# Three self-attentions of a four-layer Perceiver kernel, laid out anew by head group and half batch

## The chip, the cores and the metric

The kernel runs on one core of a Trainium2 chip. The metric is the time of one execution on the device in microseconds (us). A profiled execution has a span, from its first to its last instruction, and a time of its own that also counts what lies around the span.

## The reference, cut to what matters

A tensor of 32 batches x 32 tokens x 128 features goes through four layers, each a cross-attention to a context of 257 tokens, a self-attention and a feed-forward block. Each self-attention has 16 heads of 8 features; it is made of the shapes below. Layer 0 has a linear attention that the change leaves alone. The three others are:

```python
# layer 1: causal, 16 query heads, 4 key and value heads; x normalised before
# layer 2: attends over the head axis in a transposed reading ("pairs"): tokens and
#          features are regrouped first; a relative position bias is ADDED TO THE PROBABILITIES
# layer 3: plain softmax attention; a second layer norm of the already normalised x
#          is added to the result with the projection's bias
s = einsum('bhqd,bhkd->bhqk', q, k) * 8 ** -0.5   # + causal mask in layer 1
p = softmax(s)                                     # + relative bias in layer 2
o = einsum('bhqk,bhkd->bhqd', p, v) @ Wo           # + residual
```

All of it is in float32.

## The kernel before, in words

The 1024 token rows live as 8 tiles of 128 rows (X, XN, Y, Z, ACC), and transposed, features by tokens, as XNT, ZT and OT. PSUM is one tile PS of 8 banks of 512 columns. Each engine has its own program (`@block.tensor`, `.scalar`, `.vector`, `.gpsimd`, `.sync`), written out by hand; a named semaphore in `sig` stands between every producer and consumer, and a `Tally` counts what each engine waits for. So the order of the work on an engine is exactly the order of the calls. There is no planner.

A self-attention in the token layers starts from the layer norm of the carried sum in banks 6 and 7 (`norm` on ACT for the tiles 0 to 3, `layernorm` on DVE for 4 to 7), eight transposes (`turn`, line 440) and two copies to XNT, the first half by ACT and the second by DVE. Then:

- PE projects queries and keys 512 columns at a time (`wide`, line 464) and values by token tile (line 818). ACT copies all three out of PSUM (lines 1035, 1289, 1291).
- `heads` on DVE spreads the queries: for each batch the 32 queries are written four times, masked by head, so that a group of four heads (32 rows) makes 4 x 32 columns.
- `core` on PE (line 794) makes the scores: for each half (16 batches), head group g of four and batch one 32x32 stationary of keys against 128 columns of queries. 128 matmuls; PE issues each float32 matmul as two records.
- The scores stand keys by queries. `core` on DVE transposes them in 32x32 blocks (line 1831), adds the mask, takes the maximum, subtracts; ACT takes the exponential of a half (2048 columns); DVE sums, divides (POOL does half of it in `divide`, line 2276), transposes back (lines 1859, 1870).
- `core` on PE (line 805) multiplies the values, 128 matmuls of 32x32 by 128 columns, into all eight banks; ACT and DVE pick each head out of its four (line 1877) and ACT copies to OT (lines 1271, 1278). Only then PE carries X into banks 6 and 7 (`carry`, line 456) and projects (line 472).

In the pair attention ACT stages q, k and v (1024 columns each), SP and ACT send 16 transfers to another layout (`to_pairs`, 8 each), ACT copies the parts (line 1382), `core(pairs=True)` runs, and 16 transfers bring the result back (`to_tokens`, on ACT, SP and POOL). While the first transfers are under way DVE builds the relative bias from one-hot rows (line 2097 and the products before it). In layer 3 DVE also makes the second norm between the transposes and `heads` (lines 2165 to 2171).

## Time and profile before

| | us |
|---|---|
| median of 3 runs (1364.64 to 1371.31) | 1369.34 |
| profiled execution, its own time | 1370.04 |
| its span | 1368.2 |
| PE busy in it | 1136.3 |
| DVE busy | 772.6 |
| ACT busy | 593.1 |
| POOL busy | 327.8 |

PE is TensorE's matmul records, PEld its weight loads, which overlap them; DVE is VectorE, ACT ScalarE, POOL GpSimd, SP the queue of transfers. Matmuls are pipelined and their ends are modelled, so a busy PE need not be at its peak. The mean granted clock of TensorE is 0.884 of full speed; it has two levels, 1.2 and 2.4 GHz, shown as 0.50 and 1.00. L794 is line 794 of the kernel before.

### The profile page before, as it was taken

How to read it: one execution, taken by the hardware profiler on the slowest of the kernel's cores; microseconds unless marked ns; L12 is line 12 of the kernel's file. 1: busy time of each engine (PE TensorE's matmuls, PEld its weight loads, DVE VectorE, ACT ScalarE, POOL GpSimd, SP SyncE). 2: the span in 40 equal slices, each digit the busy share in tenths (PEclk: the TensorE clock that was granted, in tenths of full speed). 3: DMA queues.
4: the chain of work that ended last, by engine and by line, in shares of the span. 5: the costliest groups of instructions: out<-in, count | busy, mean ns of one | idle time of the engine just before them, and what ended most of it. 6: DMA issues, size and time to landing. Idle time of an engine off the chain costs nothing.

```text
span 1368.2 us, 26696 instructions
## 1 busy us (share of the span) xinstructions
PE 1136.3 (83%) x8831; PEld 834.3 (61%) x8831; DVE 772.6 (56%) x2093; ACT 593.1 (43%) x1233; POOL 327.8 (24%) x504
## 2 busy tenths in 40 slices
PE   5768998999998368899986046799999989999538
PEld 2435665877785345688864034577777768887435
DVE  2375445555553953687775495534334357776783
ACT  2153223433433223677764212544344347776223
POOL 1010001112120004455531010304041315554110
PEclk8587999999999578999997556899999999999658
DMA  8510111222230002355510301021211211111000
GB/s 284 144 62 1 36 58 28 58 59 53 54 72 1 1 1 87 85 151 152 142 58 1 46 1 39 24 58 47 58 47 47 58 36 28 31 31 36 2 1 16
DMA packets 71006, 75.05 MB, mean 55 GB/s; under 512 B 6288, under 2 KB 63712, under 8 KB 70552
## 3 DMA queue, kind: packets, MB, share of 16 engines
q1 hardware_dynamic: 67880, 66.18, 17.9%
q0 software_dynamic: 1152, 6.97, 1.4%
q10 hardware_dynamic: 1904, 0.98, 0.5%
q8 instruction: 43, 0.70, 0.2%
q14 instruction: 27, 0.22, 0.1%
HBM read 71.49 MB, written 0.52 MB: 53 GB/s over the span
## 4 chain that ended last, share of the span: by engine, by line
PE 74%; DVE 14%; ACT 5%; DMA 3%; issue 2%; ACTq 1%; POOL 1%; SPq 0%; DVEq 0%; POOLq 0%
PE PS L487 13%; PE PS L499 12%; PE PS L877 9%; PE PS L717 4%; PE PS L887 4%; DVE AR L1436 4%; PE PS L681 4%; PE PS L464 2%; PE PS L724 2%; PE PS L668 2%; PE PS L490 2%; PE PS L860 2%; PE PS L867 2%; PE PS L907 2%; PE PS L440 2%
## 5 line engine op out<-in xcount | busy, mean ns | idle before, releaser
L499 PEld LDWEIGHTS PS<-WB,AR 128*128 128x128 f32 x1568 | 190.5, 193 | 43.6 <-issue 38.8
L499 PE MATMUL PS<-WB,AR 128*128 128x128 f32 x1568 | 190.7, 276 | 0.0
L1035 ACT ACTIVATE AR<-PS,WB 128x512 f32<-128x512 f32 x160 | 110.0, 687 | 155.0 <-PE PS L487 148.2
L877 PE MATMUL PS<-AR 128*128 128x257 f32 x512 | 138.6, 393 | 1.7 <-POOL AR L2307 1.6
L1561 DVE SCALAR_TENSOR_TENSOR ACC<-PS,SM,ACC 128x128 f32<-128x128 f32 x192 | 54.1, 345 | 95.1 <-PE PS L499 94.1
L487 PE MATMUL PS<-ZT,WB 128*128 128x512 f32 x208 | 100.9, 608 | 0.3 <-ACT AR L1035 0.3
L877 PEld LDWEIGHTS PS<-AR 128*128 128x128 f32 x512 | 87.1, 190 | 21.4 <-issue 7.2
L1436 DVE TENSOR_TENSOR AR<-PS,AR 128x512 f32<-128x512 f32 (+2 forms) x69 | 48.4, 701 | 90.1 <-issue 39.3
L487 PE MATMUL PS<-XNT,WB 128*128 128x512 f32 x168 | 89.1, 638 | 5.2 <-ACT AR L1035 4.1
L1035 ACT ACTIVATE AR<-PS 128x512 f32<-128x512 f32 (+2 forms) x82 | 44.3, 541 | 112.9 <-PE PS L490 68.0
L1035 ACT ACTIVATE AR<-PS,SM 128x257 f32<-128x257 f32 x136 | 64.6, 475 | 38.7 <-DVE SM L1644 28.8
L1561 DVE SCALAR_TENSOR_TENSOR X<-PS,SM,X 128x128 f32<-128x128 f32 x168 | 47.2, 344 | 59.2 <-PE PS L499 58.8
L805 PE MATMUL PS<-AR 32*32 32x128 f32 x768 | 31.4, 374 | 58.0 <-DVE AR L1870 57.5
L887 PE MATMUL PS<-W,AR 128*128 128x128 f32 x512 | 76.8, 273 | 1.5 <-ACT AR L1035 1.4
L1035 ACT ACTIVATE AR<-AR 128x1024 f32<-128x1024 f32 (+1 forms) x39 | 46.3, 1188 | 71.2 <-DVE AR L1436 56.1
L887 PEld LDWEIGHTS PS<-W,AR 128*128 128x128 f32 x512 | 63.4, 141 | 15.1 <-ACT AR L1035 2.6
L2307 POOL TENSOR_TENSOR AR<-AR,W 128x512 f32<-128x512 f32 x64 | 67.0, 1047 | 19.9 <-POOL OT L2335 13.4
L1035 ACT ACTIVATE AR<-AR,SM 128x257 f32<-128x257 f32 x128 | 65.3, 510 | 14.7 <-DVE SM L1983 9.4
L2257 POOL TENSOR_TENSOR AR<-AR,SM 128x516 f32<-128x516 f32 x32 | 33.7, 1054 | 156.8 <-ACT SM L1035 93.9
L794 PE MATMUL PS<-AR 32*32 32x128 f32 x768 | 27.9, 416 | 47.0 <-DVE AR L1436 45.9
L440 PE MATMUL PS<-W,XN 128*128 128x128 f32 x96 | 29.7, 397 | 44.6 <-ACT XN L1035 44.3
L805 PEld LDWEIGHTS PS<-AR 32*32 32x32 f32 x768 | 26.2, 147 | 63.5 <-DVE AR L1870 61.0
(266 smaller groups left out, 2246.0 us busy)
## 6 DMA issues: line engine op xcount, KB each, us to landing
WB<-in_units SPq DMA_DIRECT2D x49, 385.0 KB, 3.1
CTX<-in_fside SPq DMA_DIRECT2D x32, 514.0 KB, 4.1
CTX<-in_ctxT SPq DMA_DIRECT2D x96, 130.0 KB, 2.1
CTX<-in_ctxT SPq DMA_DIRECT2D x8, 520.0 KB, 4.8
CTX<-in_ctxN SPq DMA_DIRECT2D x16, 258.0 KB
CTX<-in_ctxN SPq DMA_DIRECT2D x32, 129.0 KB, 2.3
AR<-in_ctxN SPq DMA_DIRECT2D x32, 64.5 KB, 2.9
AR<-in_l1x_w POOLq DMA_DIRECT2D x1, 2048.0 KB, 8.4
```

What stands on the lines that cost most here:

```text
L440: m = pe.transpose(PS[:, t // 4, 128 * (t % 4):128 * (t % 4) + 128], src[:, t, :], ident)
L487: m = pe.matmul(bank(2 * c), WB[:, q, 128 * c:128 * c + 128], src[:, 512 * hh:512 * hh + 512], start=True, stop=True)
L499: m = pe.matmul(PS[:, 4 + hh, 128 * t:128 * t + 128], f_h[hh][:, c, 128 * t:128 * t + 128], WB[:, q, 2 * UNIT + 128 * c:2 * UNIT + 128 * c ...
L681: m = pe.matmul(bank(1 + c), c_T[k][:, P * c:P * c + P], rhs, start=True, stop=True)
L717: m = pe.matmul(o, y_P[q][:, c, P * g:P * g + P], c_N[k][:, c, :], start=(c == 0), stop=(c == 1))
L805: m = pe.matmul(PS[32 * g:32 * g + 32, 4 * half + b, P * tt:P * tt + P], c_vt[32 * b:32 * b + 32, at:at + 32], pt[32 * b:32 * b + 32, g, t ...
L877: m = pe.matmul(PS[:, 2 + g, 0:KEYS], x_qb[q][:, P * g:P * g + P], x_k[q], start=True, stop=True)
L887: m = pe.transpose(PS[:, 6 + pair, 256 * c + P * (g % 2):256 * c + P * (g % 2) + P], x_p[q][:, g, P * c:P * c + P], ident)
L1035: return act.activation(o, i, fn, **k)
L1436: return dve.tensor_tensor(o, a, b, op)
L1561: ins = dve.scalar_tensor_tensor(out=a, in0=y, scalar=f_w[:, 4 * hh + t, bass.ds(e, 1)], in1=a, op0=ALU.mult, op1=ALU.add)
L2307: pool.tensor_tensor(x_qb[q].rearrange("p (h q) -> p h q", h=H), qv, m16, ALU.mult)\
```

## The change

Scores are made queries by keys, so that a row of PSUM is a query and the softmax runs along rows with no 32x32 transposes. For that the keys, not the queries, are spread by head (ACT copies with a scale column, `c_keys`). The work is cut into 8 units u: a half of the batches and a head group, 512 columns each. DVE takes maximum and difference straight out of PSUM, ACT the exponential, DVE the sums; PE transposes the unit in four 128x128 steps (`c_turn`), ACT copies it. Values are projected per batch and head (`c_values` on PE), spread to a block form by POOL (`spread_values`), and PE weighs them with the turned exponentials (`c_weigh`). The division comes last: the reciprocals are transposed and spread by PE over the output's layout (`c_turn_sums`, `c_spread`) and DVE multiplies (`c_close`). The causal mask is written by PE into PSUM before the scores add to it. The bias of the pair attention becomes a product of its own (`c_pair_bias`) from a table that POOL builds early. The second norm of layer 3 is derived from the first one's variance, and its tiles are made by POOL. The engines' orders, from the diff:

```diff
+            def c_scores(half, query, causal):
+                ...
+                def hide(g):
+                    r = slice(32 * g, 32 * g + 32)
+                    for b in range(4):
+                        pe.matmul(out(b, g).rearrange("p (m k) -> p m k", k=32), ident[r, r],
+                                  w("causal")[r].unsqueeze(1).broadcast_to([32, 16, 32]), start=True, stop=False,
+                                  skip_group_check=True)
+                ...
+                            n = 16 * half + 4 * tt + b
+                            m = pe.matmul(out(b, g)[:, P * tt:P * tt + P], query(n)[r], c_kb[r, P * n:P * n + P],
+                                          start=not causal, stop=True, skip_group_check=True)
+            def c_values(half, source, weight):
+                by_head = weight.rearrange("p (g h d) -> p h g d", g=HG, h=4)
+                for i in range(16):
+                    for h in range(4):
+                        m = pe.matmul(PS[32 * h:32 * h + 32, 6 + half, 32 * i:32 * i + 32]
+                                      .rearrange("p (g d) -> p g d", g=HG),
+                                      source(16 * half + i), by_head[:, h], start=True, stop=True,
+                                      skip_group_check=True)
+            def c_turn(u, to=None):
+                pe.wait_ge(sig["c_exp"], seen.up("c_exp"))
+                for tt in range(4):
+                    m = pe.transpose(PS[:, u if to is None else to, P * tt:P * tt + P], c_p[u][:, P * tt:P * tt + P],
+                                     ident)
+            def c_weigh(u):
+                half = u // 4
+                pe.wait_ge(sig["c_pt_taken"], seen.up("c_pt_taken", 2))
+                if u % 4 == 0:
+                    pe.wait_ge(sig["c_vb_ready"], seen.up("c_vb_ready"))
+                for i in range(16):
+                    tt, b = i // 4, i % 4
+                    for v in (u, u + 1):
+                        g = v % 4
+                        at = P * (16 * half + i) + 32 * g
+                        m = pe.matmul(PS[32 * g:32 * g + 32, 4 * half, 32 * i:32 * i + 32], c_vb[:, at:at + 32],
+                                      c_pt[v][:, P * tt + 32 * b:P * tt + 32 * b + 32], start=True, stop=True,
+                                      skip_group_check=True)
```

PE's order in the token attentions, with K and Q for the wide projections of a half:

```
turn(XN) K0 Q0 scores(0) K1 Q1 c_turn(0) values(0) c_turn(1) values(1) scores(1)
c_turn(2) weigh(0) c_turn(3) c_turn(4) weigh(2) turn_sums(0) c_turn(5) spread(0) c_turn(6)
carry X half 0, weigh(4) c_turn(7) carry X half 1, project half 0, turn_sums(1) weigh(6) spread(1) project half 1
```

ACT's: keys(0), X half 0, exp(0), keys(1) heads 0 and 1, exp(1), heads 2 and 3, queries of half 1, then copies of the turned units, values and exponentials in PE's order. In the pair attention PE makes both halves' values first, then all scores, then c_turn(0) to (3), weigh(0), c_turn(4), weigh(2), pair_bias(0), turn_sums(0), c_turn(5), spread(0), c_turn(6), weigh(4), c_turn(7), pair_bias(1), turn_sums(1), weigh(6), spread(1); ACT's and DVE's loops there and the staging are:

```diff
-            for k, c in enumerate("qkv"):
+            for k in (0, 2):
+                if k:
+                    act.wait_ge(sig["lin_ready"], seen.up("lin_ready", 2))
...
+            for u in range(8):
+                c_exp(u)
+                c_turned(u)
+                if u == 4:
+                    c_weighed(0)
+                    c_sums(0)
+            c_sums(1)
+            c_weighed(1)
...
+                for u in range(8):
+                    c_shift(u)
+                    if u:
+                        c_sums(u - 1)
+                c_close(0, pairs)
+                c_sums(7)
+                c_close(1, pairs)
```

POOL in layer 3 makes Z in three passes over 128x1024 before `spread_values`, and adds it to X after:

```diff
+            pool.tensor_tensor(Z[:, :, :], XN[:, :, :], second.unsqueeze(2).broadcast_to([P, NT, P]), ALU.mult)\
...
+            spread_values()
             pool.wait_ge(sig["x_half_a"], 5)
             pool.wait_ge(sig["x_half_d"], 5)
...
             pool.tensor_tensor(X[:, :, :], X[:, :, :], Z[:, :, :], ALU.add).then_inc(sig["bias_ready"], 1)
```

## Rows read from the trace of the kernel before

**Rows 1.** Page, busy time by engine and the chain by engine.
```profile
PE 1136.3 (83%) x8831; PEld 834.3 (61%) x8831; DVE 772.6 (56%) x2093; ACT 593.1 (43%) x1233; POOL 327.8 (24%) x504
...
PE 74%; DVE 14%; ACT 5%; DMA 3%; issue 2%; ACTq 1%; POOL 1%; SPq 0%; DVEq 0%; POOLq 0%
```

**Rows 2.** Windows, first self-attention: length, busy us per engine (count), granted clock, DMA.
```profile
449.00:458.00 9.00, 8.94 (x256) 8.32 (x256) 8.66 (x11) 0.00 (x0) 0.00 (x0) 0.50 0.01 4
458.00:476.00 18.00, 0.00 (x0) 0.00 (x0) 17.52 (x15) 3.82 (x2) 0.79 (x1) 0.50 0.00 0
```

**Rows 3.** Chain of waits, first self-attention (start us, us, what); first of five.
```profile
462.93 2.33 DVE AR L1831
```

**Rows 4.** Timeline, ends of both token stages: start, us, engine, line, operation [idle].
```profile
437.40 0.60 ACT L1035 ACTIVATE XNT<-PS 128x512 f32<-128x512 f32 x1 [0.48 <-PE PS L440]
...
498.04 0.89 DVE L1440 BATCH_NORM_STATS2 ST<-PS 128x6 f32<-128x128 f32 x4 [5.40 <-PE PS L472]
...
1270.76 0.60 ACT L1035 ACTIVATE XNT<-PS 128x512 f32<-128x512 f32 x1 [0.48 <-PE PS L440]
...
1336.18 0.89 DVE L1440 BATCH_NORM_STATS2 ST<-PS 128x6 f32<-128x128 f32 x4 [6.36 <-PE PS L472]
```

**Rows 5.** Timeline, pair attention: staging, first transfer, data used, transfers back.
```profile
752.96 3.40 ACT L1035 ACTIVATE AR<-PS,W 128x1024 f32<-128x1024 f32 x3 [5.97 <-PE PS L464]
...
779.65 5.97 ACT L1382 COPY AR<-AR 128x1024 f32<-128x1024 f32 x3 [23.28 <-DMA AR<-AR]
...
832.48 4.01 SPq L414 DMA_DIRECT2D ZT<-OT  x5
```

**Rows 6.** Timeline, ACT, DVE and POOL on 128x512 in the first self-attention.
```profile
452.72 0.69 DVE L1837 TENSOR_REDUCE SM<-AR 128x16 f32<-128x512 f32 x1
...
475.21 3.02 POOL L2276 TENSOR_TENSOR AR<-AR,SM 128x512 f32<-128x512 f32 x2 [58.55 <-DVE SM L1848]
...
481.22 0.69 ACT L1035 ACTIVATE AR<-PS,W 128x512 f32<-128x512 f32 x1 [7.00 <-PE PS L805]
```

**Rows 7.** Timeline of PE, runs by shape; two groups of the page.
```profile
23.12 1.08 PE L560 MATMUL PS<-CTX,AR 128*32 128x257 f32 x8
24.09 1.66 PE L581 MATMUL PS<-CTX,AR 128*32 128x128 f32 x24
...
600.58 0.32 PE L902 MATMUL PS<-AR,W 128*32 128x64 f32 x8
600.71 0.62 PE L907 MATMUL PS<-AR 128*32 128x128 f32 x16
...
602.23 0.60 PE L887 MATMUL PS<-W,AR 128*128 128x128 f32 x4
...
784.11 4.86 PE L794 MATMUL PS<-AR 32*32 32x128 f32 x128 [31.25 <-DVE AR L1436]
...
788.90 1.97 PE L784 MATMUL PS<-W,AR 128*128 128x128 f32 x8
...
832.51 3.78 PE L456 MATMUL PS<-Y,W 128*128 128x512 f32 x4 [5.45 <-ACT OT L1278]
...
874.28 1.88 PE L487 MATMUL PS<-XNT,WB 128*128 128x512 f32 x4
...
L887 PE MATMUL PS<-W,AR 128*128 128x128 f32 x512 | 76.8, 273 | 1.5 <-ACT AR L1035 1.4
...
L794 PE MATMUL PS<-AR 32*32 32x128 f32 x768 | 27.9, 416 | 47.0 <-DVE AR L1436 45.9
```

**Rows 8.** Timeline: POOL's longest wait, DVE's second norm.
```profile
223.73 2.35 POOL L2217 TENSOR_TENSOR X<-X,RB 128x1024 f32<-128x1024 f32 x1 [131.51 <-DVE XN L1466]
...
1282.27 0.20 DVE L2168 RECIPROCAL SD<-SD 128x8 f32<-128x8 f32 x1 [6.55 <-ACT SD L1035]
```

**Rows 9.** Windows where the granted clock had changed.
```profile
439.00:440.00 1.00, 1.00 (x2) 0.56 (x2) 0.92 (x2) 0.99 (x2) 0.00 (x0) 0.50 0.00 0
...
480.00:482.00 2.00, 1.12 (x48) 0.85 (x40) 1.97 (x2) 0.69 (x1) 0.00 (x0) 1.00 0.00 0
```

More of the change, by code:

```diff
@@ new lines, in c_turn_sums, with c_spread @@
+            def c_turn_sums(half):
+                pe.wait_ge(sig["c_rec"], seen.up("c_rec"))
+                pe.transpose(PS[0:64, 4 * half + 1, 0:P], c_sum[half], ident).then_inc(sig["c_rec_turned"], 1)
+            def c_spread(half):
+                pe.wait_ge(sig["c_rec_taken"], seen.up("c_rec_taken"))
+                if half == 0:
+                    pe.wait_ge(sig["c_select"], seen.up("c_select"))
+                for tt in range(4):
+                    m = pe.matmul(PS[:, 4 * half + 1, P * tt:P * tt + P], c_select[0:64, P * tt:P * tt + P],
+                                  c_recT[half][0:64, :], start=True, stop=True, skip_group_check=True)
+                m.then_inc(sig["c_spread"], 1)
@@ new lines, in out_taken, with fill, project_half @@
+            def out_taken(hh):
+                pe.wait_ge(sig["c_out"], seen.up("c_out"))
+            def fill(hh, src):
+                pe.matmul(bank(6 + hh), ident, flat(src)[:, 512 * hh:512 * hh + 512], start=True, stop=False,
+                          skip_group_check=True)
+            def project_half(hh, weight):
+                for t in range(4 * hh, 4 * hh + 4):
+                    m = pe.matmul(PS[:, 6 + hh, P * (t % 4):P * (t % 4) + P], OT[:, P * t:P * t + P], weight,
+                                  start=False, stop=True, skip_group_check=True)
+                m.then_inc(sig["proj_ready"], 1)
@@ new lines, in self_attention, with one @@
+            def self_attention(q, k, v, o, wrote, causal, bias=None):
+                kq_waits.update(ck_taken=(0, 1), cq_taken=(1,), cq_taken_d=(0,))
+                query = lambda n: c_q[:, 32 * n:32 * n + 32]
+                token = lambda n: XNT[:, 32 * n:32 * n + 32]
+                def one(k, hh, name, weight):
+                    pe.matmul(bank(k), weight, XNT[:, 512 * hh:512 * hh + 512], start=True, stop=True)\
+                        .then_inc(sig[name], 1)
+                turn(XN)
+                half_taken(0)
+                one(4, 0, "ck_ready", w(k))
+                one(5, 0, "cq_ready", w(q))
+                half_taken(1)
+                c_scores(0, query, causal)
+                one(4, 1, "ck_ready", w(k))
+                one(5, 1, "cq_ready", w(q))
+                c_turn(0)
+                x_written(0, wrote)
+                c_values(0, token, w(v))
+                c_turn(1)
+                x_written(1, wrote)
+                c_values(1, token, w(v))
+                c_scores(1, query, causal)
+                c_turn(2)
+                c_weigh(0)
+                c_turn(3)
+                c_turn(4)
+                c_weigh(2)
+                c_turn_sums(0)
+                c_turn(5)
+                c_spread(0)
+                c_turn(6, 2)
@@ new lines, in c_keys @@
+            def c_keys(half, heads, ready=None):
+                if ready:
+                    act.wait_ge(sig[ready], seen.up(ready))
+                dst = c_kb[:, 2048 * half:2048 * half + 2048].rearrange("p (n h k) -> p h n k", n=16, h=4)
+                for h in heads:
+                    ins = f(dst[:, h], PS[:, 4, :].rearrange("p (n k) -> p n k", n=16), scale=w("mask4")[:, h:h + 1])
+                    name = "ck_taken" if h == 3 else "act_ran"
+                    ins.then_inc(sig[name], 1)
+                    act.wait_ge(sig[name], seen.up(name))
@@ L1283, in self_attention, with c_values @@
+            def c_values(half):
+                act.wait_ge(sig["cv_ready"], seen.up("cv_ready"))
+                act.copy(c_vc[:, 512 * half:512 * half + 512], PS[:, 6 + half, :]).then_inc(sig["cv_taken"], 1)
+                act.wait_ge(sig["cv_taken"], seen.up("cv_taken"))
             def self_attention(scale, second_norm=False):
                 norm(carried_tile, XN)
-                turned(XNT[:, :], None if second_norm else ACT.Exp, True)
-                act.wait_ge(sig["lin_ready"], seen.up("lin_ready"))
@@ L1298, in self_attention @@
-                core()
+                turned(XNT[:, :])
+                if second_norm:
+                    act.wait_ge(sig["second_var"], 1)
+                    f(second, second, ACT.Sqrt, bias=eps_col).then_inc(sig["second_std"], 1)
+                    act.wait_ge(sig["second_std"], 1)
+                prepare(ACT.Exp)
+                c_keys(0, range(4), "ck_ready")
+                act.copy(flat(X)[:, 0:512], PS[:, 6, :]).then_inc(sig["x_half_a"], 1)
+                act.wait_ge(sig["x_half_a"], seen.up("x_half_a"))
@@ L1896, in _ @@
             layernorm(carried_tile, XN, True)
             turned(XNT[:, :], True)
-            dve.wait_ge(sig["w_l1"], 16)
-            heads()
-            core("causal")
+            attend()
             layernorm(carried_tile, XN, True)
```

542 lines of the change are left out of this document (300 added, 242 removed).

## The prediction, made before the changed kernel was run

> **What bounds the kernel now.** I read the page first: PE is busy for 83% of the span and carries 74% of the chain that ended last, DVE 14% [rows 1]. That is an average. The change touches three stages only, so each was read by itself in the windows and in the chain of waits. In the first self-attention PE works 8.94 of 9 us on the scores, then for 18 us not at all while DVE is busy for 17.52, then partly again beside a busy DVE [rows 2]. The chain there is DVE: five passes in a row over 128x2048, 2.3 us each, the first at 462.93 [rows 3]. So the three stages are bound by DVE after their scores, and the 74% says nothing about them.
>
> Their lengths, from timeline marks. Token attentions: from the first half of XNT written to the first statistics of the next norm: 438.00 (437.40 + 0.60) to 498.04, 60.0 us; 1271.36 (1270.76 + 0.60) to 1336.18, 64.8 us [rows 4]. The pair attention: ACT starts staging at 752.96 and the transfers to pairs follow when it ends, at 756.36; the data are used from 779.65, the transfers back are issued at 832.48: 52.8 us from landed to issued, and 3.4 us of staging [rows 5]. Together 177.6 us of the 1368.2.
>
> **The change part by part.** After it DVE has per unit of 512 columns one maximum and one subtraction out of PSUM and one sum: 8 x 3 passes of 512 columns, 0.69 us each over SBUF [rows 6] and up to 0.75 from PSUM, and little else, some 20 us in the stage in place of some 50. ACT gets 8 key copies, 8 exponentials, 8 copies of turned tiles and 8 others at about 0.65 (0.69) [rows 6], some 20 us. POOL spreads the values, 2 x 128x2048; four times 1.45 us each (3.02 for two of 128x512) [rows 6], 5.8 us a half, in time both times for the weighing. What grows is PE: beside the 128 score matmuls (two records each) it now does 128 for the values by head (128 rows, 32 columns stationary, 32 moving), 128 to weigh them, 32 transposes of 128x128 for the probabilities, two spreads of the reciprocals, and in the causal stage 32 matmuls of 512 columns for the mask; the pair stage gets 128 more for its bias in place of 8 transposes. PE becomes the bound, so I sum PE.
>
> Prices per record [rows 7]. Small tile (32 columns): at half clock the scores took 8.94 us for 256 records [rows 2], 0.035 each. A run's time less the last record's own (0.42 at half, 0.27 at full clock, the means 416 and 273 in rows 7), over the others' count, is the distance of two. At the full clock 16 records of 128x32 with 128 moving columns took 0.62: (0.62 - 0.27)/15 = 0.023; I take 0.024. The trace has none with 32 moving columns. Bounds: below, 8 records with 64 columns in 0.32 at full clock, less 0.22 over 7, 0.014 (0.027 at half); above, 24 of 128x32 at half clock, 1.66 less 0.42 over 23, 0.054 (0.033 at full, the score rate unchanged by the clock). I take 0.035 and 0.024, since the scores are the one long unbroken run of small tiles, as the new ones are. Transposes: 8 records in 1.97, less 0.42 over 7, 0.21 at half; 4 in 0.60, less 0.27 over 3, 0.11 at full. 512 columns: 4 records in 3.78 at half (0.85) and 1.88 at full (0.43). A change of tile shape: the scores of 784.11 end at 788.97, so the last began at 788.55, and the transposes begin at 788.90: 0.35 for a step that is 0.035 inside the run, so some 0.30; at full I take 0.17.
>
> So, half clock / full clock: scores of a half 64 x 2 x 0.035 = 4.5 / 3.1; values of a half 4.5 + 0.3 = 4.8 / 3.2; weighing two units 64 records, 2.5 / 1.7; turning one unit 8 x 0.21 + 0.3 = 2.0 / 1.05; two wide projections 3.4 / 1.7; spread 2.0 / 1.05; turning the sums 0.6 / 0.47.
>
> The new order has some 18 changes of shape per stage where the old had 2; at 0.30 / 0.17 they are 5.4 / 3.1 us of each stage's sum. The Trainium skill, TensorEngine Tiling (Array Packing), Key Properties, says that a change of the tiling mode, and not of the tile, drains the engine. The row agrees, and it speaks against this change: without such a drain each of the three stages would be shorter by the amount just given, and the forecast 9 us earlier.
>
> Third-layer stage. Keys spread by ACT before the first scores: 1.91 for the matmul, 0.36 until seen, four copies of 0.72: 5.2. Scores 4.5, projections of the second half 3.4, turn 2.0, values 4.8, all at half clock: 19.9. Then second turn, second values, second scores. Then the tail: six turns, four weighings, two spreads, two turned sums, two carries of X, one half of the output projection, and 1.6 to evict and multiply. At half clock: 11.2 and 32.6 + 1.7, so 19.9 + 11.2 + 34.3 = 65.4, less overlaps 64.8 when the four queues are laid out in program order, each instruction starting when its engine is free and what it waits for is there ("walked" from here on); at full clock after the first values 7.4 and 18.9 + 1.5, so 47.6, walked 47.2. The second norm's DVE work (some 5 us from 1282.27 on) [rows 8] goes out of the chain and is 7 to 10 us on POOL; hidden, since X is carried at 37 us into the stage and POOL ends at 36. If that cover goes, it costs what it is late.
>
> First stage (causal): mask matmuls 8 x 4 x 2 records, 257 columns gave (1.08 - 0.60)/7 = 0.069 at half, so 0.12 for 512 and half that at full; the first 32 mostly lie beside the key copies. Walked: 49.8 with the full clock from the second turn on, 67 if it holds only until the second scores end, 71 at half clock.
>
> Pair stage. q, k and v are staged as each is ready, k by DVE beside ACT: first issue 2.3 us sooner. The DVE work on the bias (products and sums over the one-hot rows) stood beside the transfers, which take until 779.65 [rows 5], and was free; on POOL it is some 22 us early in the kernel, where POOL waits 131 us before 223.73 [rows 8]: nothing either way, and if that cover goes nobody needs it before 780. From landed: values wait 1.5 for POOL's copy, then values 4.8 + 3.2, scores 3.1 + 4.5: 17.1. Then ACT takes in order the exponential of unit u and the copy of the turned unit u, so PE and ACT alternate: 2.0 + 0.36 + 0.64 + 0.66 = 3.7 a unit for four units, with PE idle for 1.7 of it. Then four weighings 10.2, four turns 7.9, bias 2 x 4.8, sums and spreads 5.2 with 1.4 for the sums' way through ACT, close 2.0. Walked 66.3. So 66.3 - 2.3 - 52.8 = +11.2. At full clock it is 47.4, -7.7.
>
> **Which clock.** This decides between -48 and +25 us. The trace: granted 0.50 from 439 on, right after eight transposes with gaps between them [rows 9]; during the 32x32 scores it stayed at 0.50 for all of 9 us at 99% busy [rows 2], though the 32x32 value products, which use four strips of rows and not one, brought it to 1.00 by 480-482 [rows 9]. The new values and weighing use all 128 rows. I take: half clock until the first values have run, full from there in the two token stages, where PE never stops; in the pair stage half in the tail, since PE stands for 1.7 of every 3.7 us at its start. Sum: 49.8 - 60.0 = -10.2; 47.2 - 64.8 = -17.6; +11.2. Total -16.6 on the profiled execution's 1370.04 us (span 1368.2): 1353.4. That execution stands 0.7 over the median of 1369.34; I say 1353.
>
> **Rivals.**
> *Full clock throughout* the three stages: walked 42.9, 41.1 and 47.4 - 2.3: -17.1, -23.7, -7.7 = -48.5, 1321. For it: PE has no long pause. Against: scores at 0.50 for 9 us, transposes before the half clock at 439. Chance 0.2.
>
> *Slower: the tail falls to 1.2 GHz and stays there.* The second scores run row strip by row strip, as the ones that never raised the clock [rows 2]; after them transposes fill half of PE's time, and the clock fell after transposes at 439 [rows 9]. Then the stages take 67.0 and 60.9, the pair stage 66.3 - 2.3: +7.0, -3.9, +11.2 = +14.3, 1384; with everything at half clock +10.9, 0, +14.1 = +25, 1395. It decides where the slower clock costs more than the 16.6 us that the forecast gains, 8.3 in each token stage; the walk has 17.2 and 13.7. Chance 0.27. The Trainium skill, TensorE: Matmul & The Clock Gate, Part 4, says that transposes do not count as work for the clock as matmuls do; by that rule this rival gains, and the trace agrees so far as the window from 439 shows it.
>
> *Small tiles dearer than their price.* With 0.054 / 0.033 for values, weighing and bias, and the clock as forecast: 55.7, 53.1, 79.6 - 2.3: -4.3, -11.7, +24.5 = +8.5, 1378; half way to it 1366, which is no change. With the lower bound -30, 1340. Chance of the dear one 0.11.
>
> **How the numbers follow.** Forecast 0.42, full clock 0.2, slower 0.27, dear tiles 0.11. Faster by over 0.5% (6.8 us, about what can be told from no change) holds for the forecast in 95 of 100, for the full clock always, for dear tiles in 3 of 10: 0.63. Within 0.5%: 0.09. Slower: nearly all of the third case and the rest: 0.28. The range goes from the full clock (1321) to the first form of the slow rival: 1320 to 1386; the forecast's own is 1335 to 1368.
>
> **What would show it.** Right: PE busy over 90% in both token stages, DVE under half; stages of 50, 47 and 64 us; granted clock 1.00 in the weighing of the token stages; PE with gaps of 1 to 2 us between turns in the pair stage. Wrong: granted clock 0.50 in that tail (slow rival); weighing records over 0.04 apart at full clock (dear tiles); a wait of PE for POOL's values or for the carried X (POOL becomes the bound); a pair stage under 53 us.

## The result, and the profile after

The changed kernel took 1322.66 us, the median of 4 runs (1318.34 to 1324.02), beside 1369.09 for the kernel before on the same chip: a ratio of 0.966 (95% interval 0.963 to 0.969), 46.4 us less. The forecast was 1353, a gain of 16.6. A second measurement beside other kernels (f1) gave 0.966 again. The direction was right and the gain almost three times the forecast. The time is that of the "full clock" rival (1321), but the clock stood at 0.50 for parts of all three stages, so what that rival says did not happen either, and its hitting the time is luck.

The page of the kernel after: busy time, and the chain of waits by engine.

```profile
PE 1150.5 (87%) x10033; PEld 843.7 (64%) x10033; DVE 691.6 (52%) x2019; ACT 612.3 (46%) x1286; POOL 380.5 (29%) x551
...
PE 78%; DVE 7%; ACT 5%; DMA 4%; issue 2%; POOL 1%; ACTq 1%; SPq 1%; DVEq 0%; POOLq 0%
```

DVE lost 81 us of busy time (772.6 before), PE gained 14.2. The windows of the first self-attention, as in [rows 2] (length, busy us of each engine, granted clock, DMA share, GB/s):

```profile
442.98:450.00 7.02, 5.79 (x166) 3.46 (x165) 3.44 (x6) 4.82 (x8) 0.00 (x0) 1.00 0.01 2
450.00:458.00 8.00, 6.59 (x284) 4.34 (x280) 6.09 (x10) 7.00 (x11) 1.20 (x1) 1.00 0.02 4
458.00:466.00 8.00, 8.00 (x133) 4.96 (x129) 4.18 (x7) 1.22 (x3) 7.86 (x2) 0.51 0.02 4
466.00:474.00 8.00, 7.99 (x174) 6.62 (x165) 3.15 (x5) 3.54 (x6) 0.00 (x0) 0.63 0.01 2
```

In the last 9.68 us of the stage the granted clock is 1.00 again. From the first half of XNT to the next statistics, PE is busy for 36.8 of 40.7 us and DVE for 21.2: the bound has moved from DVE to PE. The ends of the stages, timeline of ACT, DVE, POOL and SP, as in [rows 4, 5]:

```profile
442.38 0.60 ACT L1182 ACTIVATE XNT<-PS 128x512 f32<-128x512 f32 x1 [0.48 <-PE PS L451]
...
483.68 0.49 DVE L1632 BATCH_NORM_STATS2 ST<-PS 128x6 f32<-128x128 f32 x2
...
742.56 5.60 SPq L422 DMA_DIRECT2D AR<-AR  x8
...
765.87 2.94 POOL L2559 COPY AR<-AR 128x512 f32<-128x512 f32 x2 [30.11 <-DMA AR<-AR]
...
809.77 3.15 SPq L425 DMA_DIRECT2D ZT<-OT  x4
...
1249.67 0.60 ACT L1182 ACTIVATE XNT<-PS 128x512 f32<-128x512 f32 x1 [0.48 <-PE PS L451]
...
1289.45 0.69 DVE L1632 BATCH_NORM_STATS2 ST<-PS 128x6 f32<-128x128 f32 x3
```

| us | before | forecast | after | moved |
|---|---|---|---|---|
| first self-attention (442.98 to 483.68) | 60.0 | 49.8 | 40.7 | -19.3 |
| third layer's (1250.27 to 1289.45) | 64.8 | 47.2 | 39.2 | -25.6 |
| pair attention, landed to issued (765.87 to 809.77) | 52.8 | 66.3 | 43.9 | -8.9 |
| staging of the pairs, from the projection's first matmul to the first issue | 10.8 | 8.5 | 7.8 | -3.0 |
| transfers back, issue to PE's use | 7.0 | 7.0 | 10.0 | +3.0 |
| first feed-forward block | 110.4 | 110.4 | 117.8 | +7.4 |

These make -46.4; the two profiled executions, from which they are read, differ by 46.0 (1370.04 and 1324.02). The block in the last row goes from the statistics of one norm (107.47 before, 106.91 after) to those of the next (217.85 and 224.69); POOL's table of the pair bias runs in it. In other profiled runs of kernels that leave the first self-attention as it is, that stage lay between 40.3 and 43.3 us, so a difference under 3 us in this stage says little. The third layer's lay between 39.6 and 40.6 in such runs and the pair stage between 43.1 and 43.7.

PE's runs in that stage, timeline (start, us, engine, line, operation, shape, count [idle before, and what ended it]); L830 turns a unit, L820 makes values, L811 scores, L855 weighs:

```profile
447.43 2.76 PE L811 MATMUL PS<-AR 32*32 32x128 f32 x128 [1.23 <-ACT AR L1182]
...
451.94 0.60 PE L830 MATMUL PS<-W,AR 128*128 128x128 f32 x4
452.47 1.30 PE L820 MATMUL PS<-W,XNT 128*32 128x32 f32 x128
453.69 0.66 PE L830 MATMUL PS<-W,AR 128*128 128x128 f32 x4
454.28 1.20 PE L820 MATMUL PS<-W,XNT 128*32 128x32 f32 x117
456.89 0.32 PE L820 MATMUL PS<-W,XNT 128*32 128x32 f32 x11 [1.41 <-issue]
...
467.43 1.11 PE L830 MATMUL PS<-W,AR 128*128 128x128 f32 x4
468.47 1.92 PE L855 MATMUL PS<-AR 128*32 128x32 f32 x64
...
472.17 1.21 PE L855 MATMUL PS<-AR 128*32 128x32 f32 x64
```

And in the pair attention:

```profile
767.41 3.30 PE L820 MATMUL PS<-W,AR 128*32 128x32 f32 x226 [25.65 <-POOL AR L2559]
772.17 0.65 PE L820 MATMUL PS<-W,AR 128*32 128x32 f32 x30 [1.45 <-issue]
772.75 9.35 PE L811 MATMUL PS<-AR 32*32 32x128 f32 x256
782.03 1.11 PE L830 MATMUL PS<-W,AR 128*128 128x128 f32 x4
784.53 1.11 PE L830 MATMUL PS<-W,AR 128*128 128x128 f32 x4 [1.39 <-ACT AR L1182]
```

Three things are to be seen. A unit's turn is 4 records, 0.60 to 0.66 us at a granted 1.00 and 1.11 at 0.50; the forecast has 8 records, 1.05 and 2.0. A run of 128 value records takes 1.30 us at 1.00, 0.009 us a record, and 226 take 3.30 at 0.50, 0.0145; the forecast has 0.024 and 0.035. And the long runs of narrow records are broken by pauses of 1.41 and 1.45 us that end in "issue": PE waited for nothing that the profile shows.

### The profile page after: what moved, and what is told of

It is laid out like the page before. It is cut to its first block, busy times and chain, and to the rows that moved or that the text cites. A ratio compares the mean times of both kernels' runs of the same rounds, so it can differ in the third digit from the quotient of the medians.

```text
span 1322.2 us, 29209 instructions
## 1 busy us (share of the span) xinstructions
PE 1150.5 (87%) x10033; PEld 843.7 (64%) x10033; DVE 691.6 (52%) x2019; ACT 612.3 (46%) x1286; POOL 380.5 (29%) x551
## 4 chain that ended last, share of the span: by engine, by line
PE 78%; DVE 7%; ACT 5%; DMA 4%; issue 2%; POOL 1%; ACTq 1%; SPq 1%; DVEq 0%; POOLq 0%
PE PS L498 13%; PE PS L510 13%; PE PS L1021 9%; PE PS L728 4%; PE PS L1031 4%; PE PS L692 4%; DMA CTX<-in_ctxT 2%; PE PS L501 2%; PE PS L679 2%; PE PS L735 2%; PE PS L1004 2%; PE PS L811 2%; PE PS L1051 2%; PE PS L1011 2%; ACT AR L1182 2%
## 5 line engine op out<-in xcount | busy, mean ns | idle before, releaser
L510 PEld LDWEIGHTS PS<-WB,AR 128*128 128x128 f32 x1568 | 189.5, 192 | 43.7 <-issue 40.2
L1628 DVE TENSOR_TENSOR AR<-PS,AR 128x512 f32<-128x512 f32 (+2 forms) x71 | 49.8, 701 | 97.3 <-ACT AR L1182 41.0
L498 PE MATMUL PS<-XNT,WB 128*128 128x512 f32 x168 | 90.5, 646 | 10.2 <-DVE AR L1628 6.0
L1182 ACT ACTIVATE AR<-PS,SM 128x257 f32<-128x257 f32 x136 | 64.8, 476 | 39.8 <-DVE SM L1836 30.2
L1753 DVE SCALAR_TENSOR_TENSOR X<-PS,SM,X 128x128 f32<-128x128 f32 x168 | 47.2, 344 | 57.9 <-PE PS L510 57.6
L1182 ACT ACTIVATE AR<-AR,SM 128x257 f32<-128x257 f32 x128 | 65.4, 511 | 15.4 <-DVE SM L2151 10.3
L728 PE MATMUL PS<-CTX,AR 128*128 128x129 f32 x512 | 62.4, 275 | 0.0
L2473 POOL TENSOR_TENSOR ACCB<-RB,SM 128x1024 f32<-128x1024 f32 x5 | 9.6, 1914 | 183.0 <-DVE SM L1628 183.0
L692 PE MATMUL PS<-AR,CTX 128*128 128x512 f32 x128 | 60.4, 594 | 0.8 <-ACT AR L1342 0.8
L1182 ACT ACTIVATE AR<-AR 128x1024 f32<-128x1024 f32 (+1 forms) x57 | 50.0, 877 | 22.9 <-DVE AR L1957 13.8
```

The lines of the kernel that those rows point to most:

```text
L498: m = pe.matmul(bank(2 * c), WB[:, q, 128 * c:128 * c + 128], src[:, 512 * hh:512 * hh + 512], start=True, stop=True)
L510: m = pe.matmul(PS[:, 4 + hh, 128 * t:128 * t + 128], f_h[hh][:, c, 128 * t:128 * t + 128], WB[:, q, 2 * UNIT + 128 * c:2 * UNIT + 128 * c ...
L692: m = pe.matmul(bank(1 + c), c_T[k][:, P * c:P * c + P], rhs, start=True, stop=True)
L728: m = pe.matmul(o, y_P[q][:, c, P * g:P * g + P], c_N[k][:, c, :], start=(c == 0), stop=(c == 1))
L1182: return act.activation(o, i, fn, **k)
L1628: return dve.tensor_tensor(o, a, b, op)
```

## The experiments

Each edit is one to the kernel after, and stage lengths are compared with its own (40.7, 39.2, 43.9 for first, third, pair). All were timed beside the kernel before on their chip; ratios are to that. e1 and f2 ask what POOL's table costs. e3, e2 and e13 price the new records by doing them twice, and e10 and e11 look into PE's pauses. e6 and e7 are about the clock, e4 and e12 about the order of the scores, e5 and e9 about ACT and DVE, and e8 and e14 put edits together.

**e1, f2: the table waits for the gates.**

```diff
             normed(4)
+            pool.wait_ge(sig["expert_weights"], at_gates)
             pair_bias_table()
```

> One wait is added: POOL starts the pair bias table only when DVE has finished the gates of the first feed-forward stage; the work itself stays. Theory (contention): POOL's 27 us of table work from 116 on lie beside DVE's small gate instructions, which took 0.97 to 2.15 us in place of 0.20 in the kernel after; behind the gates PE is the bound, so the work costs nothing there. The stage from the second norm's statistics to the next ones falls from 117.8 to about 110.4, the time from 1322.7 to about 1315.3. Rival: the stage is longer for another reason (the order of PE or the loads); then it stays at 117.8 and the time at 1323. Second rival: the table only moves its harm, into the experts' part, where DVE stands at half busy: 113 to 118.

The stage fell from 117.8 to 110.2. DVE's gate instructions in the kernel after, and then in e1 (timeline of DVE):

```profile
120.61 0.97 DVE L1931 COPY SM<-SM 128x64 f32<-128x64 f32 x1 [2.71 <-ACT SM L1182]
...
125.79 2.15 DVE L1934 TENSOR_SCALAR SM<-SM 128x64 f32<-128x64 f32 x1
127.97 1.34 DVE L1628 TENSOR_TENSOR SM<-SM 128x64 f32<-128x64 f32 x1
```

```profile
120.71 0.20 DVE L1931 COPY SM<-SM 128x64 f32<-128x64 f32 x1 [2.72 <-ACT SM L1182]
...
124.57 0.20 DVE L1934 TENSOR_SCALAR SM<-SM 128x64 f32<-128x64 f32 x1
124.80 0.22 DVE L1628 TENSOR_TENSOR SM<-SM 128x64 f32<-128x64 f32 x1
```

The same copy of 128x64 takes 0.97 and 0.20, the same tensor_scalar 2.15 and 0.20; the chain of gates, 10.2 us beside the table (120.61 to 130.79), takes 5.5 without it. That is 4.7 of the 7.6 us. The rest is PE's clock. PE's first matmuls of the experts behind the gates, and the instruction of POOL that lies beside the long tensor_scalar (timeline of POOL and PE in the kernel after, then of PE in e1):

```profile
125.56 2.32 POOL L2415 TENSOR_TENSOR ACC<-W,ACCB 128x1024 f32<-128x1024 f32 x1
131.53 2.07 PE L498 MATMUL PS<-XNT,WB 128*128 128x512 f32 x2 [5.99 <-DVE AR L1628]
```

```profile
126.92 1.12 PE L498 MATMUL PS<-XNT,WB 128*128 128x512 f32 x2 [1.29 <-DVE AR L1628]
```

Behind a wait of 5.99 us PE works at a granted 0.54 from 131 to 138; behind one of 1.29 it stays at 1.00. From there to the next statistics it is 93.9 us in the kernel after and 91.0 in e1, with the same 421 matmul records. The Trainium skill, SBUF — State Buffer, 🔬 SBUF: two separate sides, says that VectorE and GpSimd hold a shared pair of ports as a lock for a whole instruction; the trace agrees in so far as the tensor_scalar that takes 2.15 ends at 127.94, with the instruction of POOL beside it (127.88), while a reduction, with one input, kept its 0.69. The ratio, 0.9655 (0.962 to 0.969), did not tell this from the kernel after, so it was timed again on one chip with it:

> As e1_table_late, beside the changed kernel on the same chip. Theory (the table costs what the stage in the trace shows): 7.6 us under f1. Rival (the rest of the kernel gives part of it back, a ratio of 0.9655 against 0.9659): 0 to 3 us under f1.

1318.6 (ratio 0.962, 0.960 to 0.964) beside 1324.0 (0.966, 0.964 to 0.968) for the changed kernel: 5.5 us. The table costs 5 to 8 us, not nothing.

**e3: turns done twice.**

```diff
-                for tt in range(4):
+                for tt in (0, 1, 2, 3) * 2:
                     m = pe.transpose(PS[:, u if to is None else to, P * tt:P * tt + P], c_p[u][:, P * tt:P * tt + P],
```

> Every transpose of the probabilities is done twice (4 more per unit, 24 units). Theory (a transpose is one record, 0.15 us at 2.4 GHz, 0.27 at 1.2): +0.6 per unit in the token stages at full clock, +1.1 at half and in the pair stage: +5 to +6 for each token stage, +7 to +8 for the pair stage, together +17 to +20. Rival (two records each at the forecast's 0.11 and 0.21): +0.9 and +1.7 per unit, together +27 to +32. If the clock falls to 0.50 for the whole tail because more transposes stand in it, the token stages rise by 8 and more each.

1327.4 (0.971, 0.966 to 0.975), +4.8: both were too high. The doubled turns at either level of the clock, timeline of PE:

```profile
451.01 1.04 PE L830 MATMUL PS<-W,AR 128*128 128x128 f32 x8
...
463.96 1.97 PE L830 MATMUL PS<-W,AR 128*128 128x128 f32 x8
```

Four transposes more add 0.43 us at 1.00 (1.04 to 1.09 in place of 0.60 to 0.66) and 0.86 at 0.50 (1.97 in place of 1.11): 0.11 and 0.21 a record, the forecast's own prices. In the kernel after what follows a turn starts 0.49 to 0.59 us behind its start at 1.00 and 1.04 at 0.50, so a change of shape costs 0.05 to 0.15 and 0.20 there, under the forecast's 0.17 and 0.30. Wrong was the count: it gave a transpose two records, as a matmul has, though the eight transposes of the pair stage before stand as x8 in [rows 7]. By stage: third +5.4, pair +4.8, first -0.8, where the clock stood at 0.50 for 7 us and not for 14, behind a pause of 0.82 and not 1.41. These make +9.4, but that profiled execution is only 3.1 us longer; the rest of it, which the edit leaves alone, was 6 us shorter, so the price is read from the stages.

**e2: values done twice.**

```diff
-                for i in range(16):
+                for i in list(range(16)) * 2:
                     for h in range(4):
```

> Every matmul that makes the values of a half is done twice (64 more matmuls, 128 records, per half; 6 halves), the output is the same. It prices the narrow record that the forecast had no row for. Theory (cheap records, 0.010 us at 2.4 GHz and 0.0145 at 1.2, as the spacing in the kernel after shows, and PE is the bound): +1.3 per half in the token stages, +1.9 per half in the pair stage, together +9; no more if the end of a run of records is only modelled too early. Rival 1 (the forecast's 0.024 and 0.035): +3.1 and +4.5 per half, together +21. Rival 2 (PE is not the bound there): under +4.

1346.3 (0.984, 0.982 to 0.986): +24, against my theory (+9) and past rival 1 (+21). First stage +9.8 (8.6 of it from the first value record to the first mask), third +8.3, pair +6.0. PE in the first stage, then the transfers of the stretch from 448 to 468 (GB/s in 40 slices of 0.5 us):

```profile
452.14 2.49 PE L820 MATMUL PS<-W,XNT 128*32 128x32 f32 x249
457.07 0.27 PE L820 MATMUL PS<-W,XNT 128*32 128x32 f32 x7 [2.44 <-issue]
457.27 0.66 PE L830 MATMUL PS<-W,AR 128*128 128x128 f32 x4
457.86 1.80 PE L820 MATMUL PS<-W,XNT 128*32 128x32 f32 x117
461.08 1.94 PE L820 MATMUL PS<-W,XNT 128*32 128x32 f32 x128 [1.43 <-issue]
465.08 0.43 PE L820 MATMUL PS<-W,XNT 128*32 128x32 f32 x11 [2.07 <-issue]
```

```profile
GB/s 0 0 0 0 33 0 0 0 0 0 0 0 33 0 0 0 0 0 0 0 33 0 0 0 0 0 0 0 0 33 0 0 0 0 0 0 0 33 0 0
...
q8 instruction: 5, 0.08, 1.9%
```

After some 250 narrow records PE runs 128, stops, runs 128 again: the pauses end at 457.07, 461.08 and 465.08, 4.0 us apart. In the same stretch a packet of 16 KB of the instruction queue starts every 3.7 to 4.6 us. So a long run of narrow records goes at 128 in 4.0 us, 0.031 a record, here at a granted 0.50, where a short one went at 0.0145.

**e13: the weighing done twice.**

```diff
-                for i in range(16):
+                for i in list(range(16)) * 2:
                     tt, b = i // 4, i % 4
                     for v in (u, u + 1):
```

> Every weighing matmul is done twice: 64 records more in each of 12 weighings, 768 in all, as many as in e2_values_twice (+24 us), but in runs of 128 with transposes or wide records between them. Theory (short runs are fed from what has already been fetched: 0.016 to 0.018 us a record at 2.4 GHz, 0.026 at 1.2): +1.1 for nine or ten weighings and +1.7 for the others, together +13 to +16. Rival 1 (the added records cost the supply's 0.031 wherever they stand): +24. Rival 2 (the forecast's 0.024 and 0.035): +20.

1338.6 (0.977, 0.975 to 0.979): +16, as the theory had it. As many records of the same shape as in e2 cost a third less where other work stands between them: +4.5 and +2.6 in the token stages, in place of 9.8 and 8.3, but +6.4 in the pair stage, no less than in e2. A weighing of 128 records takes 2.22 us at 1.00 where one of 64 takes 1.21, so 0.016 a record.

**e10 and e11: half the values, and wide records between.**

```diff
-                    for h in range(4):
+                    for h in range(2):
```

> The values are made for heads 0 and 1 of each sequence only, 32 matmuls (64 records) a half in place of 64 (128); what belongs to heads 2 and 3 is left out of the values. Doubling them cost 4.0 us for each 128 records in the first token stage (9.8 for 256), though 128 took 1.30 once in the kernel after, and PE had pauses of 2.44, 1.43 and 2.07 us in those runs that end with nothing that the profile shows. Theory (after some 250 records in a row PE waits for its own instructions, which come in steps): with half of them the pauses of 1.41 (first stage), 1.20 + 0.89 (third) and 1.45 (pair) go as well: -2.5 to -3 a token stage, -2.5 pair, together -7 to -9. Rival (a record costs 0.010 and the pauses have another cause, such as the copies of the values): -1.3 a token stage, -1.9 pair, together -4.5.

1317.1 (0.962, 0.958 to 0.966). Stages -6.2, -1.4, -0.6 = -8.2; the pauses of the token stages are gone. Most of the first stage's gain is not the records: its second scores kept the full clock until about 463 and took 6.0 us in place of 10.3. The pair stage gained 0.6 where the theory said 2.5, since PE then waited 3.14 us for POOL, which spreads the keys of the second half (line 2565).

```diff
+                if half:
+                    for j in range(2):
+                        pe.matmul(bank(7), ident, XNT[:, 0:512], start=True, stop=True)
                 for i in range(16):
```

> Two matmuls of 512 columns (4 records, 1.88 us at 2.4 GHz, 3.78 at 1.2) are added ahead of the second half's values in all three stages. Theory (PE's pause behind some 250 narrow records is the time in which the next instructions arrive): the wide records fill the pause: first stage +0.5 in place of 1.9, third about 0, pair +2.3 in place of 3.8; together +3. Rival (the pause is tied to something else, or PE's rate alone counts): +1.9, +1.9, +3.8, together +7.6.

> As e11_wide_between, beside the changed kernel on the same chip. Theory (the wide matmuls fill PE's pauses and the clock stays up longer in the second scores): the stages' -2.6, -0.7 and +0.4, about 3 us under f1 though work is added. Rival (nothing that can be told): within 2 us of f1.

Work was added and the kernel did not get slower: stages -2.6, -0.7, +0.4 and a time of 1320.6 (0.964, 0.960 to 0.968); f3 1322.1 beside f1's 1324.0, intervals that overlap (0.962 to 0.966 and 0.964 to 0.968). The rival's +7.6 is out. The first stage took 38.1 and 38.3 us in the two, under the 40.3 to 43.3 of the kernels that leave it alone. The first stage's pause is gone, and where the kernel after stood at 0.56 the clock is still granted. Windows of 458 to 460 in the kernel after and in e11:

```profile
458.00:460.00 2.00, 2.00 (x44) 1.45 (x40) 0.32 (x2) 1.22 (x3) 2.00 (x1) 0.56 0.04 8
```

```profile
458.00:460.00 2.00, 2.00 (x72) 1.37 (x66) 1.22 (x2) 0.47 (x1) 2.00 (x1) 1.00 0.00 0
```

In e10 and e11 the first stage's pause goes when there are fewer narrow records or wide ones between, which is what a wait for instructions does. The traces say more. In the traces of the kernel after and of the 17 runs told of here PE has 98 pauses of over 0.4 us in the three stages that end in "issue"; every one of them ends 1.2 to 1.6 us after a packet of 16 KB of the instruction queue has landed, though the packets start 3.2 us apart or more. The one at 456.89 ends 1.40 us after the packet of 454.52 to 455.48. No semaphore ties the two, so that the packets are what releases PE stays an inference, one that the times and both edits support.

**e6 and e7: dense matmuls while PE waits for the pairs**, 14 and 28.

```diff
+                for i in range(14):
+                    pe.matmul(bank(1), ident, XNT[:, 0:512], start=True, stop=True)
                 for half in range(2):
                     pe.wait_ge(sig["pair_v"], half + 1)
```

> Added work: 14 matmuls of 512 columns into an unused bank while PE waits 25.6 us for the transfers to pairs (741.8 to 767.4), nothing else changed. At 0.50 they take at most 24 us, so they delay nothing. Theory (the pair stage is long because the clock stands at 0.50 from landing to 792): it begins at granted 1.00; values 1.3 in place of 3.3 and 0.65, 256 score records 5.5 in place of 9.3, turns 0.66 in place of 1.1: up to -8 us, pair stage 36 to 38. Rival (the clock falls again with the first narrow records, as it did at 459 in the first stage after 20 us at 1.00, or the narrow records do not follow the clock): -0 to -2.5 us.

> As e6_dense_before with 28 matmuls in place of 14: there the 14 took 12.2 us at 1.00, PE then stood still for 13.4 us and the granted clock was back at 0.50 when the values began, so the question stayed open. 28 take 24.4 us at 1.00 and end within a us of the landing. Theory (the clock is kept by what PE did just before): the values run at 1.00 (1.3 us a half in place of 3.3), and the first scores as well; pair stage 38 to 41 in place of 43.9. Rival (the narrow records draw the clock down at once): values 2.9 to 3.3 and a pair stage of 43 to 44.

e6 ended 13.4 us too early and the clock was back at 0.50: no answer (1321.5; 0.968, 0.965 to 0.970; pair stage 42.4). e7 (1325.4, 0.969, 0.967 to 0.972) gives it, by timeline of PE:

```profile
767.78 1.30 PE L820 MATMUL PS<-W,AR 128*32 128x32 f32 x128 [1.18 <-POOL AR L2561]
769.25 0.58 PE L820 MATMUL PS<-W,AR 128*32 128x32 f32 x42 [0.17 <-POOL AR L2561]
771.19 0.95 PE L820 MATMUL PS<-W,AR 128*32 128x32 f32 x86 [1.36 <-issue]
772.06 1.11 PE L811 MATMUL PS<-AR 32*32 32x128 f32 x41
774.76 7.73 PE L811 MATMUL PS<-AR 32*32 32x128 f32 x215 [1.58 <-issue]
```

The values run at 1.00, 128 in 1.30 us, and it gains nothing: the pauses come sooner and are as long (1.36 and 1.58), the clock then falls to 0.50 in the scores (7.73 for 215), and landed to issued is 44.8. A full clock ahead of a long narrow run is no gain here. The values went as the theory said, the stage as the rival.

**e4 and e12: strips of rows interleaved in the scores**, two at a time, and all four (e12 on top of e8).

```diff
-                for g in range(HG):
...
+                            for g in (g0, g0 + 1):
+                                r = slice(32 * g, 32 * g + 32)
```

> Only the order of the score matmuls changes: the two units of a pair of head groups are interleaved, so that neighbouring records use different strips of 32 rows, and the first unit of each pair is told to DVE together with the second. Theory A (the strips of columns already overlap and a record costs what it costs): spacing 0.0195 us per record at 2.4 GHz and 0.036 at 1.2 GHz stay, and each half loses up to 0.7 us for the later first unit: 0 to +3 us in all. Theory B (records in different strips of rows overlap as well): the spacing falls to 0.010 to 0.015, a half's scores from 2.8 to 4.0 us to 1.4 to 3, and the granted clock may stay at 1.00 in the second scores of the first stage, where it fell to 0.50: -4 to -12 us. The forecast had taken the strip-by-strip order as what holds the clock down; if that is so, the granted clock from 459 to 472 rises here.

> As e8_three, with all four strips of rows interleaved in the scores. With two, 128 records took 2.05 us at 2.4 GHz in place of 2.76 and 3.54 at 1.2 in place of 4.0 to 4.6. Theory (strips of rows overlap further): 1.5 and 2.5, less up to 1.5 us a half for DVE's later start: -3 to +3 against e8_three's 1304.2. Rival (the supply of instructions, 128 records per 4 us in a long run, is now the bound): no shorter than with two strips, and later for DVE: +3 to +6, 1307 to 1310.

e4: 1317.2 (0.962, 0.959 to 0.965). Its first scores, timeline of PE:

```profile
449.49 2.05 PE L813 MATMUL PS<-AR 32*32 32x128 f32 x128 [1.23 <-ACT AR L1185]
```

128 score records in 2.05 us in place of 2.76 at 1.00, 3.54 in place of 4.6 at 0.50; stages -3.9, +0.3, -2.0. Theory B, at its lower end. The Trainium skill, TensorE: Matmul & The Clock Gate, The mechanism (Part 3), says that a weight load overlaps with a running matmul only if its group of rows is another; the trace agrees in its direction, 0.0195 us a record strip by strip and 0.014 with two interleaved. Whether it is the whole reason isn't shown. The clock fell in the second scores as before (0.50 from 461 to 470). e12 (0.954, 0.949 to 0.959) can't be told from e8 (1304.3 and 1304.2): the first scores took 1.90 and the clock stayed at 1.00 in the whole first stage (34.6 us), though not in the third (0.50 from 1246 to 1255). The pair stage gained nothing (37.4 against 36.6): its scores were as long, since PE's pauses that end in "issue" grew from 3.4 us in all to 6.4 and its waits for POOL's keys from 0.31 to 0.85.

**e5: ACT's exponential first.**

```diff
+            c_exp(0)
             for u in range(8):
-                c_exp(u)
+                if u < 7:
+                    c_exp(u + 1)
                 c_turned(u)
```

> Pair stage alone: ACT takes the exponential of unit u+1 ahead of the copy of the turned unit u. In the kernel after the first four turns start 2.51 us apart (782.10, 784.53, 787.04, 789.55) of which PE works 1.13. Theory (the ping-pong of PE and ACT is what sets this stretch): they come 1.3 to 1.5 us apart, the pair stage falls from 43.9 to about 39.5, the time by 4 us. Rival (DVE, which follows the exponentials with sums, maxima and subtractions at 2.1 us a unit, takes the place): they come 2.1 apart after the third, gain 1 to 2 us. The forecast's way of laying out gave for the same change about -5.

1317.8 (0.963, 0.960 to 0.966). Timeline of PE, where the turns start at 782.68:

```profile
782.68 1.97 PE L830 MATMUL PS<-W,AR 128*128 128x128 f32 x8
785.18 1.11 PE L830 MATMUL PS<-W,AR 128*128 128x128 f32 x4 [0.54 <-ACT AR L1182]
786.46 1.11 PE L830 MATMUL PS<-W,AR 128*128 128x128 f32 x4 [0.17 <-ACT AR L1182]
```

The first two turns now form one run of 1.97 us and the next start 1.28 apart; the pair stage took 37.8, -6.1, more than the theory's 4.4, since the later units gain as well.

**e9: DVE's sums done twice.**

```diff
+                for twice in range(2):
                     dve.tensor_reduce(by[:, 16 * (u % 4):16 * (u % 4) + 16], ...
```

> DVE sums the exponentials of every unit twice (24 more passes over 512 columns, 0.69 us each, 17 us of DVE's time in all). Theory (PE and its supply set the three stages, DVE stands at half busy): the token stages take 0 to 2 us more each, the pair stage, where each shift waits behind the sum of the unit before, 0 to 5; together +2 to +8. Rival (DVE still sets them, as in the kernel before): +5.5 a stage, +17.

1324.1 (0.966, 0.962 to 0.970), +1.4 where the rival said +17: +0.6, +1.0, +0.9 in the stages for 5.5 us of DVE each. DVE no longer bounds any of them.

**e8 and e14: together.** e8 has the edits of e1, e5 and e4, as shown; e14 has e11's as well.

> The table behind the gates, ACT's exponential ahead of the turned copy in the pair stage, and the scores with two strips of rows interleaved, together. If they are independent, what each gave alone adds up: -7.6 (table, 110.2 in place of 117.8), -6.1 (pair stage 37.8 in place of 43.9), -5.6 (strips: -3.9 first token stage, -2.0 pair, +0.3 third): the time 1303 in place of 1322.7. Rival: DVE, which starts later with interleaved scores, becomes the bound of the pair stage once PE no longer waits for ACT; then the strips' 2.0 there are lost and the time is 1306.

> e8_three with the two wide matmuls ahead of the second half's values as well. In e11 they took 2.6 and 0.7 us off the token stages (they filled pauses of 1.41 and 1.20 us, and the second scores ran longer at 1.00) and added 0.4 to the pair stage. Theory (the two do not touch each other): -3 against e8_three, 1301. Rival (with interleaved strips the scores are too short for the clock to matter, and the pauses only move to the scores): 0 to +3, 1304 to 1307.

e8: 1304.2, ratio 0.952 (0.949 to 0.956), the sum of its parts. e14: 1302.9, 0.951 (0.949 to 0.954), faster than both kernels; from e8 it can't be told. Its token stages took 34.4 and 35.6 us, where e8's took 37.5 and 39.2.

## Why the prediction was wrong in size

Right: that DVE bounds the stages before and PE after (e9); the alternation of PE and ACT in the pair stage, with PE idle for 1.39 before each turn against the "1 to 2"; 0.11 and 0.21 for a transpose; the second norm hidden; the sign. Nearly right: PE busy for 90% of the first stage and 86% of the third, where over 90% was said, and DVE for 52% and 56%, where under half was said. Of the signs of being wrong one came true: the pair stage was under 53 us.

Wrong, by step:

- *"turning one unit 8 x 0.21 + 0.3 = 2.0 / 1.05"*: a transpose is one record and not two. A unit measured 1.11 / 0.66. Laid out in program order as in the forecast, with nothing else changed, this shortens the three stages by 3.5, 2.7 and 6.7. (Figures from laying out, here and below, are estimates; no run shows them by themselves.)
- *"I take 0.035 and 0.024, since the scores are the one long unbroken run of small tiles, as the new ones are"*: this is the largest error. In the token stages the new runs aren't long, 64 or 128 records between wide ones. The values took 0.009 at 1.00 and 0.0145 at 0.50, under the forecast's lower bound (0.014 and 0.027); the weighing took 0.016 at 1.00 (e13), a little over it. And the scores are dear for a reason of their own, one strip of rows after another (e4). Laid out with 0.0095 and 0.0145 the stages lose another 7.9, 4.5 and 14.1; with both corrections they come to 38.4, 40.0 and 45.5, together 123.9, where 40.7, 39.2 and 43.9, 123.8, were measured and 163.3 was forecast. That it fits so well is in part luck, since 0.0095 is too little for the weighing and the pauses and the clock cancel (below). The price of 0.024 to 0.035 isn't wrong for every run: more than 250 in a row cost 0.031 (e2).
- *"half clock until the first values have run, full from there"*: first stage 1.00 until 458, 0.50 to 472, then 1.00; third 0.50 from 1257 to 1264 and from 1271 to 1277, each time over a part of the scores and what follows them, 1.00 between and after; pair 0.50 to 792, then mostly 1.00. The reading that it rests on, *"granted 0.50 from 439 on, right after eight transposes"*, is wrong as well. In the kernel before the clock was back at 1.00 from 442 to 449, and at 0.50 again when the scores began, before which PE had waited 3.69 us; the slower rival leaned on the same reading:

```profile
439.00:442.00 3.00, 3.00 (x4) 1.23 (x4) 0.92 (x2) 1.12 (x2) 0.00 (x0) 0.50 0.00 0
442.00:449.00 7.00, 3.34 (x20) 2.38 (x18) 2.37 (x2) 3.05 (x3) 0.00 (x0) 0.99 0.00 0
```

  By the same laying-out the clock as granted is worth -2.8, -0.2 and -3.0 against the clock assumed, and the pauses that the forecast didn't have are 1.4, 2.1 and 2.7: the two cancel. This was to "decide between -48 and +25", and by the laying-out it was the smallest of these three errors.
- *The pair stage, +11.2*: it came to -8.9, by the three points above. Its staging gained 3.0 (forecast 2.3), and the transfers back took it away again, 10.0 in place of 7.0. PE's timeline from the landing (765.87) to the transfers back (809.77), pauses and waits included, beside the forecast's terms, which add up to 66.8 (walked 66.3):

| us, pair stage | forecast | after |
|---|---|---|
| until the values | 1.5 | 1.5 |
| values, both halves | 8.0 | 5.3 |
| scores, both halves | 7.6 | 9.3 |
| first four turns | 14.8 | 8.6 |
| four weighings | 10.2 | 5.8 |
| last four turns | 7.9 | 3.1 |
| bias | 9.6 | 4.2 |
| sums and spreads | 5.2 | 4.1 |
| close | 2.0 | 2.0 |

  So in rows too it is the turns, 11.0 in all, and the narrow records of values, weighing and bias, 12.5, while the scores, which stood at 0.50, took 1.7 more.
- *POOL's table, "nothing either way"*: +7.4. I had asked whether POOL had time, and not what DVE does meanwhile on small instructions in the chain. These took 4.7 us more, and the clock that fell while PE waited for them most of the rest (e1).

The rivals: the slower one is out, since the token stages' tails ran at 1.00 from 472 and 1277 on, and so are the dear tiles. For the rule that transposes don't count as work for the clock, nothing here decides: with twice as many transposes the first stage stood at 0.50 for less time (e3), and in the kernel after it fell in the narrow scores.

What stays open: that the instruction packets release PE from its "issue" pauses, which only their times say; why the first stage's length varies by 3 us between runs of one kernel (in f1, with 43.3, the pause was 2.02 and the clock at 0.53 from 472 to 476, in the kernel after 1.41 and 1.00); and the transfers back, where one queue's last packet ended 6.4 us after the first issue before and 9.3 after, with the same 196,800 bytes.

## What to carry to other kernels

Price a record by the run that it will stand in, not by its shape alone: here runs of 64 to 128 between wide work were cheap, and those of more than 170 to 250 were broken by pauses. When an engine pauses for nothing that the profile names, look at the packets of the instruction queue. Count a group's records against the code's loop before dividing by it. Work moved to an idle POOL was not free where DVE was on the chain beside it, and there a wait of PE cost twice, by itself and by the clock behind it. Read the granted clock of a stretch over its whole length before naming what it followed.

## What the runs showed of the hardware that was not expected

- Narrow records (32 columns moving): 0.009 us for the values and 0.016 for the weighing in short runs at 1.00, 0.028 to 0.031 in long ones, with pauses of 0.5 to 2.4 us ending in "issue", each 1.2 to 1.6 us after an instruction packet of 16 KB landed (e2, e7 and all variants).
- Adding wide matmuls ahead of narrow ones (1.88 us in each token stage, 3.10 in the pair stage) cost nothing that can be told (e11, f3).
- Scores of 32x32 with two strips of rows interleaved: 2.05 for 128 records in place of 2.76; with four, 1.90 (e4, e12).
- DVE's 128x64 tensor_scalar: 0.20 alone, 2.15 beside POOL (e1).
- The granted clock was at 0.54 for 7 us behind a wait of PE of 5.99 us, and stayed at 1.00 behind one of 1.29 (after, e1).
